# Attention adapter: another order of the small pieces of work in each pipeline slot

## What is computed

```python
# layer 0, "the adapter": 8 heads of 20 columns
hs = mha(x @ Wq, ctx[:, :508] @ Wk, ctx[:, :508] @ Wv)
ca = ctx[:, 508:]                                  # the last 4 context rows
q1 = einsum('btc,th->bch', ca, Wq_ca)[:, indices]
hs1 = mha(q1, x, x)
hs2 = mha(hs1 @ Wq, ca @ Wk_ca, ca @ Wv_ca)
x = (hs + hs2) @ Wout + b_out + x
# layer 1: 20 heads of 64 columns
x = attn(ln(x), ln(x), ...) + x                    # "self"
x = attn(ln(x), ctx, ...) + x                      # "cross"
x = geglu_ff(ln(x), ...) + x
```

## Time and profile before

| | |
|---|---|
| median of 3 runs | 1473.61 us (1472.61 to 1474.12) |
| the profiled execution: its own time | 1475.56 us |
| the profiled execution: span | 1473.8 us |
| mean granted PE clock, whole span | 0.929 |
| adapter | 0 to 335.6 us of the span |
| steady part of the adapter | about 62 to 318 us |

### The profile page before, as it was taken

One profiled execution on the slowest core, in us unless ns is written; L12 is line 12 of the kernel. 1 busy time (PEld: TensorE's weight loads), 2 busy tenths in 40 slices (PEclk: granted clock), 3 DMA queues, 4 the chain that ended last, 5 costly groups with the idle time before them and its releaser, 6 DMA issues. The chain is left out here.

```text
span 1473.8 us, 38650 instructions
## 1 busy us (share of the span) xinstructions
PE 1360.7 (92%) x16460; PEld 1169.2 (79%) x16460; DVE 1025.4 (70%) x1902; ACT 748.2 (51%) x1356; POOL 751.0 (51%) x510
## 2 busy tenths in 40 slices
PE   4989899885999999999979999999999999999597
PEld 3777777764888898889857888888888888888587
DVE  4577777746777867786657777777777767665485
ACT  2356565552555554555425545454555555554264
POOL 2266777565434443444514545454555555455364
PEclk9588888967999999999978999999999999999699
DMA  5001110002000000000010000000010000000000
GB/s 131 12 10 46 47 32 2 2 2 65 2 2 2 2 2 2 2 2 2 2 39 7 2 7 2 7 2 7 2 45 2 2 2 2 2 2 2 12 15 23
DMA packets 31955, 20.33 MB, mean 14 GB/s; under 512 B 21414, under 2 KB 30314, under 8 KB 31786
## 3 DMA queue, kind: packets, MB, share of 16 engines
q1 hardware_dynamic: 31786, 17.86, 4.7%
HBM read 16.54 MB, written 1.31 MB: 12 GB/s over the span
## 5 line engine op out<-in xcount | busy, mean ns | idle before, releaser
L507 POOL TENSOR_TENSOR cross_probs_l<-cross_probs 128x1024 f16<-128x1024 f32 x160 | 303.6, 1897 | 276.5 <-ACT cross_probs L578 276.2
L578 ACT ACTIVATE cross_probs<-cross_score 128x1024 f32<-128x1024 f32 x160 | 163.9, 1024 | 249.9 <-PE cross_score L820 249.9
L507 POOL TENSOR_TENSOR self_probs_l<-self_probs 128x1024 f16<-128x1024 f32 x80 | 151.5, 1894 | 204.0 <-ACT self_probs L578 203.6
L675 DVE TENSOR_REDUCE cross_maxima<-cross_max 128x2 f32<-128x1024 f32 x160 | 194.6, 1216 | 7.4 <-PE cross_max L796 7.2
L1591 POOL TENSOR_TENSOR ad_probs_l<-ad_probs 128x1024 f16<-128x1024 f32 x64 | 120.8, 1893 | 97.7 <-ACT ad_probs L1668 97.0
L578 ACT ACTIVATE self_probs<-self_score 128x1024 f32<-128x1024 f32 x80 | 82.1, 1027 | 156.8 <-PE self_score L820 156.8
L840 PEld LDWEIGHTS cross_pv<-cross_v_h,cross_probs 128*128 128x128 bf16 x1280 | 116.6, 98 | 33.2 <-issue 28.2
L840 PE MATMUL cross_pv<-cross_v_h,cross_probs 128*128 128x65 bf16 x1280 | 135.3, 196 | 2.6 <-POOL cross_probs_l L507 2.6
L661 DVE TENSOR_TENSOR cross_qk_l<-cross_shared,cross_qk_h 128x256 fp32r<-128x256 f32 (+1 forms) x160 | 87.9, 556 | 69.0 <-ACT cross_qk_h L563 68.8
L841 PE MATMUL cross_pv<-cross_v_l,cross_probs 128*128 128x64 f16 x1280 | 133.9, 194 | 0.0
L842 PE MATMUL cross_pv<-cross_v_h,cross_probs_l 128*128 128x65 bf16 x1280 | 133.5, 193 | 0.0
(11 more groups left out here) (420 smaller groups left out, 4735.5 us busy)
## 6 DMA issues: line engine op xcount, KB each, us to landing
ad_ctx_rows<-in_ctx SPq DMA_DIRECT2D x8, 192.0 KB, 2.8
cross_ctx_rows<-in_ctx SPq DMA_DIRECT2D x8, 192.0 KB, 2.5
sw_raw<-in_L_xattn_wq SPq DMA_DIRECT2D x2, 640.0 KB, 6.2
sw_raw<-in_L_xattn_wk SPq DMA_DIRECT2D x2, 640.0 KB, 4.3
sw_raw<-in_L_xattn_wv SPq DMA_DIRECT2D x2, 640.0 KB, 3.8
cw_raw<-in_L_xattn_wq SPq DMA_DIRECT2D x2, 640.0 KB, 4.1
lr_raw<-in_L_xattn_w_ff SPq DMA_DIRECT2D x2, 640.0 KB
out<-x_rows SPq DMA_DIRECT2D x8, 160.0 KB, 1.9
```

Source lines behind the costliest of these rows:

```text
L507: nc.gpsimd.tensor_tensor(probs_l[:, n % PR, :, :].rearrange("p j k -> p (j k)"), whole, whole.bitcast(BF16)[:, 1::2], ALU.subtract).then_ ...
L578: nc.scalar.activation(probs[:, n % PR, :, :].rearrange("p j k -> p (j k)"), score_bank[:, :], ACT.Exp, scale=SCALE).then_inc(exped, 1)
L675: nc.vector.reduce_max(out, scores, AX.X).then_inc(max_read, 1)
```

## The change

It writes the list of a slot in another order, changes three offsets with it, and gives DVE an order of its own.

- Step 0 now holds two `weigh` groups right behind the scores, then `mt`, `e1`, `k`, `q`, `d1`. The projections come in the first half, `k` ahead of `q`.
- Step 1 begins with the other two `weigh` groups, then `top`, then all other small items, with `ctx` in slot 4b - 3 (it was 4b - 1), `x` in 4b - 4 (4b - 3), `e1` in step 0 of 4b + 9 (step 1 of 4b + 8), `e3` and `out` moved from step 0 to step 1 of their slots.
- DVE's slot is now: maximum of step 0, reads of step 0 (`k`, `q`), maximum of step 1, division, `top`, `s2`, reads of step 1.
- `find_max` waits for the read of `q` in place of `k`, since `q` is now the later one, and `KEPT` is 5.
- `DEFER` equals `SLOTS`, so that the branch `g > DEFER` is never taken: every read is done in the slot of its item.

```diff
@@ -1279,10 +1279,11 @@
     KEY_ROWS = [P] * (KT - 1) + [KEYS - (KT - 1) * P]
     ROUNDS = KT // 2
     MAX, MT, SCORE, WEIGH = 2, 3, 4, 5
-    KEPT = 4
+    KEPT = 5
     PR = 2 * ROUNDS
     UNITS = NB * APAIRS
     SLOTS = APAIRS * (NB - 1) + 11
+    DEFER = SLOTS
     SCALE = float(AD) ** -0.5
     HALF = (slice(0, P // 2), slice(P // 2, P))
     WIDE = AH * CDIM + P - CDIM
@@ -1303,38 +1304,40 @@
             if (b := batch(g, offset)) is not None:
                 out.append((step, (what, b, *n)))
 
+        def groups(step):
+            if (p := pair(g, WEIGH)) is not None:
+                out.extend((step, ("weigh", p, 2 * step + n)) for n in range(2))
+
+        groups(0)
         if (p := pair(g, MT)) is not None:
             out.append((0, ("mt", p)))
+        add(0, "e1", 9)
+        if (p := pair(g, 0)) is not None:
+            out += [(0, ("k", p)), (0, ("q", p))]
+        add(0, "d1", 7)
         add(0, "s2", 8)
-        add(0, "v", 4, 1)
-        add(0, "e3", 9)
-        add(0, "d1", 7)
-        if (b := batch(g, -1)):
-            out.append((0, ("ctx", b)))
-        add(0, "out", 10, 0)
-        add(0, "out", 10, 1)
-        if (p := pair(g, WEIGH)) is not None:
-            out += [(0, ("weigh", p, group)) for group in (0, 1)]
-        if (p := pair(g, 0)) is not None:
-            out += [(1, ("q", p)), (1, ("k", p))]
+        groups(1)
+        add(1, "top", 1, 0)
+        add(1, "top", 2, 1)
         if g < 4:
             out += [(1, key) for key in ([("w", 0), ("w", 1), ("ct",)], [("qk", n) for n in range(4)],
                                          [("g2",), ("vt",)], [("vo",)])[g]]
-        add(1, "top", 1, 0)
-        add(1, "top", 2, 1)
+        add(1, "ot", 9)
+        add(1, "v", 4, 1)
         add(1, "xv", 4)
-        if (b := batch(g, -3)):
-            out.append((1, ("x", b)))
-        add(1, "ot", 9)
-        add(1, "rows", 0)
+        add(1, "out", 10, 0)
         add(1, "mq", 3)
-        add(1, "d2", 7)
-        add(1, "v", 3, 0)
-        add(1, "e1", 8)
-        if (p := pair(g, WEIGH)) is not None:
-            out += [(1, ("weigh", p, group)) for group in (2, 3)]
         add(1, "qs", 4, 0)
         add(1, "qs", 5, 1)
+        add(1, "rows", 0)
+        if (b := batch(g, -3)):
+            out.append((1, ("ctx", b)))
+        if (b := batch(g, -4)):
+            out.append((1, ("x", b)))
+        add(1, "out", 10, 1)
+        add(1, "v", 3, 0)
+        add(1, "d2", 7)
+        add(1, "e3", 9)
         add(1, "qw", 6)
         return out
 
@@ -1726,11 +1729,11 @@
                 what, b = key[0], key[1]
                 j, bank_ = b % 2, shared[order.bank(key)]
                 if what == "q":
-                    dve.wait_ge(qk_hi, b * 2 + 1)
+                    dve.wait_ge(qk_hi, b * 2 + 2)
                     nc.vector.scalar_tensor_tensor(q_s[:, b % KEPT, :], q_t[:, :], const["low_q"], bank_[:, 0:SEQ],
                                                    ALU.mult, ALU.add).then_inc(emptied, 1)
                 elif what == "k":
-                    dve.wait_ge(qk_hi, b * 2 + 2)
+                    dve.wait_ge(qk_hi, b * 2 + 1)
                     nc.vector.scalar_tensor_tensor(k_s[:, b % KEPT, 0:KEYS], k_t[:, :], const["low_k"], bank_[:, 0:KEYS],
                                                    ALU.mult, ALU.add).then_inc(emptied, 1)
                 elif what == "x":
@@ -1850,36 +1853,52 @@
                 nc.vector.tensor_tensor(wo_a[:, 1, :], raw_o[:, 0, :], wo_a[:, 0, :], ALU.subtract)
                 nc.vector.tensor_tensor(wo_b[:, 1, :], raw_o[0:2 * HB, 1, :], wo_b[:, 0, :], ALU.subtract).then_inc(prepared, 1)
 
+            def maximum(p, step):
+                dve.wait_ge(max_filled, p * ROUNDS + step + 1)
+                nc.vector.reduce_max(maxima[:, p % 2, step, :, 0], max_bank[:, :].rearrange("p (j k) -> p j k", j=2)[:, :, 0:KEYS],
+                                     AX.X).then_inc(max_read, 1)
+
+            def normalise(p):
+                dve.wait_ge(pv_done, p + 1)
+                groups = pv_bank[:, 0:4 * AV]
+                nc.vector.reciprocal(recip[:, :], groups.rearrange("p (g d) -> p g d", d=AV)[:, :, AD]).then_inc(recip_ready, 1)
+                dve.wait_ge(recip_ready, p + 1)
+                head = p % APAIRS * 2
+                out = attn[p // APAIRS % 2][:, :, head * AD:(head + 2) * AD].rearrange("p t (h d) -> p h t d", h=2)
+                nc.vector.tensor_tensor(out, groups.rearrange("p (h t d) -> p h t d", h=2, t=QT)[:, :, :, 0:AD],
+                                        recip[:, :].rearrange("p (h t) -> p h t", h=2)[:, :, :, None].to_broadcast([P, 2, QT, AD]),
+                                        ALU.mult).then_inc(attn_ready, 1)
+
+            def units(g, step):
+                for at, key in items(g):
+                    if at != step or key[0] in ("weigh", "mt", "d1", "e1", "qs", "xv", "s2", "top"):
+                        continue
+                    if key[0] in SETUP:
+                        set_up(key)
+                    else:
+                        extra(key)
+
             def slot(g):
-                for step in range(ROUNDS):
-                    if (p := pair(g, MAX)) is not None:
-                        dve.wait_ge(max_filled, p * ROUNDS + step + 1)
-                        nc.vector.reduce_max(maxima[:, p % 2, step, :, 0], max_bank[:, :].rearrange("p (j k) -> p j k", j=2)[:, :, 0:KEYS],
-                                             AX.X).then_inc(max_read, 1)
-                    for at, key in items(g):
-                        if at != step or key[0] in ("weigh", "mt", "d1", "e1", "qs", "xv"):
-                            continue
-                        if key[0] in SETUP:
-                            set_up(key)
-                        elif key[0] == "s2":
-                            second_softmax(key[1])
-                        elif key[0] == "top":
-                            _, b, n = key
-                            dve.wait_ge(top_filled, b * 2 + n + 1)
-                            nc.vector.reduce_max(top_q[:, CDIM + 4 * n:CDIM + 4 * n + 4],
-                                                 max_bank[0:CDIM, :].rearrange("p (h k) -> p h k", h=4), AX.X).then_inc(top_read, 1)
-                        else:
-                            extra(key)
-                if (p := pair(g, WEIGH)) is not None:
-                    dve.wait_ge(pv_done, p + 1)
-                    groups = pv_bank[:, 0:4 * AV]
-                    nc.vector.reciprocal(recip[:, :], groups.rearrange("p (g d) -> p g d", d=AV)[:, :, AD]).then_inc(recip_ready, 1)
-                    dve.wait_ge(recip_ready, p + 1)
-                    head = p % APAIRS * 2
-                    out = attn[p // APAIRS % 2][:, :, head * AD:(head + 2) * AD].rearrange("p t (h d) -> p h t d", h=2)
-                    nc.vector.tensor_tensor(out, groups.rearrange("p (h t d) -> p h t d", h=2, t=QT)[:, :, :, 0:AD],
-                                            recip[:, :].rearrange("p (h t) -> p h t", h=2)[:, :, :, None].to_broadcast([P, 2, QT, AD]),
-                                            ALU.mult).then_inc(attn_ready, 1)
+
+                p = pair(g, MAX)
+                if p is not None:
+                    maximum(p, 0)
+                if g > DEFER:
+                    units(g - 1, 1)
+                units(g, 0)
+                if p is not None:
+                    maximum(p, 1)
+                if (v := pair(g, WEIGH)) is not None:
+                    normalise(v)
+                for n in range(2):
+                    if (b := batch(g, 1 + n)) is not None:
+                        dve.wait_ge(top_filled, b * 2 + n + 1)
+                        nc.vector.reduce_max(top_q[:, CDIM + 4 * n:CDIM + 4 * n + 4],
+                                             max_bank[0:CDIM, :].rearrange("p (h k) -> p h k", h=4), AX.X).then_inc(top_read, 1)
+                if (b := batch(g, 8)) is not None:
+                    second_softmax(b)
+                if g < DEFER or g == SLOTS - 1:
+                    units(g, 1)
 
             dve.wait_ge(shapes_in, 16)
             extra(("ctx", 0))
@@ -2059,7 +2078,7 @@
             def find_max(g, step, p):
                 at = p % KEPT
                 if step == 0:
-                    pe.wait_ge(emptied, order.read(("k", p)))
+                    pe.wait_ge(emptied, order.read(("q", p)))
                     after(pe, top_read, extra_fills(g, 1))
                 after(pe, max_read, p * ROUNDS + step)
                 for j, half in enumerate(HALF):
```

## The result

The changed kernel takes 1482.18 us in the median (20 runs, 1470.72 to 1488.18), the one before 1469.50 us (20 runs on the same chip, 1468.26 to 1474.26). The ratio is 1.0076, with a 95% interval of 1.0061 to 1.0092: **slower by 0.8%**, where a gain of 0.3% was forecast. The time lies within the range that was given (1453 to 1486) and beside the rival "the new stall pulls the clock down" (1482.6 us). An execution more than 1.5% above the fastest of its kernel is left out of a ratio: one of four in the second part of experiment 6, two of twelve in experiment 8. What follows compares the two profiled executions, spans of 1483.2 and 1473.8 us; their own times, 1485.02 and 1475.56 us, lie 2.8 and 6.1 us above the medians, so they differ by 9.5 us where the medians differ by 12.7. The adapter ends at 345.8 in place of 335.6 us, 10.2 us later; all that comes behind it is 0.8 us shorter.

What follows compares the result with a forecast made beforehand. No engine was taken as full: PE and DVE wait for each other in turn. The terms -20 + 14 + 2 + 1.5 - 2.5 + 0.6 = -4.4 us took 1473.6 to 1469.2 us, range 1453 to 1486.

Steps and rivals of the forecast that it cites:

- the new stall pulls the clock down: Rival: stalls before `top`, twice a batch, lower PE's clock; 9 us slower, 1482.6 us; chance 0.35.
- The sum of items 1 to 6: Whole kernel: waits removed and added come to -4.4 us, with about 32% of the stretch at 1.2 GHz.
- item 4: Weight pieces on POOL: four of seven fall into slots where POOL has little room left; +1.5 us, bounds 0 and 8.
- its deciding point, a clock of 0.81: Granted clock in the stretch where 6% more at the low level eats up the 4.4 us gain.
- A clock that leaves 0.84 by more than 0.03: Sign of being wrong: the granted clock moving that far in either direction.
- a stall above 1.6 us: Sign of being wrong: PE waiting at `top` longer than the upper bound of 1.6 us.
- PE's total idle time falls in my account: Argument against the slower case: PE, idle for 23.2 us from 62 to 318 us, would idle less.
- Item 1: PE's waits of `d2`, `e1`, `rows` and `find_max` go, `score` behind `qs` stays at 6.1 us; -20 us.
- Item 2: PE at `top` waits for the second maximum, 14 times, 1.0 us on average; +14 us, bounds +7 and +22.
- Item 3: Shorter slots of g mod 4 = 3, then the next slot's first `weigh` waits for POOL's split; +2 us.
- Items 5 and 6: The start loses `find_max` waits in slots 2 and 3, -2.5 us; at the end `e3` is read last, +0.6 us.
- "Slower": Outcome for the whole kernel: slower than before by more than about 0.2%, 3 us; chance 0.35.

Runs made afterwards that it cites:

- second part of experiment 6: Kernel before with the two `weigh` groups first in each half, nothing else moved: 1505.28 us, ratio 1.0180.
- experiment 8: Changed kernel with DVE's second maximum ahead of `k` and `q`, plus unused matmuls (five in slots with `top`, twelve with `mq`): 1465.02 us, ratio 0.9935.
- experiment 2: Changed kernel with twelve unused matmuls ahead of the last `weigh` group in slots that have a `top`: 1471.96 us, ratio 1.0000 to the kernel before.
- experiment 3: Changed kernel with the twelve unused matmuls in slots without `top` (g mod 4 = 0 and 3): 1504.53 us, ratio 1.0216 to the kernel before.
- experiment 1: Changed kernel with DVE reading the second maximum ahead of `k` and `q`: 1469.39 us, ratio 0.9989 to the kernel before.
- experiment 9: Changed kernel with DVE's second maximum ahead of `k` and `q` only in slots with `top`: 1454.18 us, ratio 0.9882 to the kernel before.
- Experiment 10: Experiment 9 with DVE's second softmax moved behind the small reads of the second half: 1451.07 us, ratio 0.9874 to the kernel before.
- experiment 4: Changed kernel with `top` as the last item of its slot on PE and DVE: 1487.65 us, ratio 1.0100 to the kernel before.
- experiment 5: Changed kernel with DVE's small reads of the second half deferred by a slot (`DEFER = 5`): 1540.00 us, ratio 1.0453 to the kernel before.

## Why the prediction was wrong

**The step that failed is the sum's clock.** The sum of items 1 to 6 leaves the share of the low clock at 32% and names its change only among the rivals. The granted clock went to 0.79. For the middle piece the shares at 1.2 GHz are 2 x (1 - 0.84) x 175.2 = 56 us before and 2 x (1 - 0.80) x 179.2 = 72 us after, for the last piece 26 and 51 us, and for the first 18 and 13 us, 35 us more in all. At the prediction's own price of 0.27 us for each, these are 9.5 us of time. Added to the forecast of -4.4 they give +5.1, and with the wait for `v`, 4.2 where item 4 had 1.5, +7.8; the adapter's end moved by 10.2, so 2.4 us stay open. The price holds on like slots of the kernel before: slot 17, with 10 us at the low clock, takes 11.5 us and slot 21, all at full clock, 8.9, which is 0.26 for each.

The rival had the mechanism, and its deciding point, a clock of 0.81, was passed. That its number is so near (1482.6 against 1482.2 us) is in part luck: it was a loss of 9 us set upon 1473.6 us for the kernel before, where the medians now differ by 12.7 upon 1469.5, and it counted on a longer stall that didn't come. A clock that leaves 0.84 by more than 0.03 and a stall above 1.6 us were the prediction's own signs of being wrong; both came. What spoke against it, "PE's total idle time falls in my account", failed: it rose from 23.2 to 27.3 us.

That the new stall is what pulls the clock down was argued there; experiments 2 and 3 show it for the middle piece. For the last piece they don't. In the changed kernel the clock falls at 310.5 us and stays low to the adapter's end, for 35 us, in the kernel before for 20; with the stall filled (2) it is still 33 us, and with it shortened 38 (1) and 34 (9). So 2 to 3.4 of the 7.6 us that the last piece loses stay when the stall is gone, and what keeps the clock low there is open. With one profile of each kernel part of it may be chance, and the changed kernel's runs do spread over 17 us.

**Item 1, waits that go (-20).** Right for `d2`, `e1` and `find_max`; and `score`, left at 6.1 us, lost most of its wait as well. Of the 23 us, 21 went, where 17 was read. But more came than items 2 to 4 held against it: 14.9 us at `top`, 4.2 for `v`, 3.2 for splits and 2.3 for the copies of `mt`, 24.6 us in place of 17.5.

**Item 2, the wait at `top` (+14, bounds 7 and 22).** Right in place, number and size: 14 waits, 14.9 us, most of them 1.0 to 1.3 us at full clock (1.2 said) and 0.3 to 0.7 at the low one (0.6 said). One, 2.30 us, passes the bound of 1.6: in slot 14 DVE reads `k` 1.33 us after the start of the second `find_max`, not 0.25, since I counted `k`'s cast from its matmuls and left out what ACT has ahead of it, here a weight piece. A stall that was forecast to 0.9 us in all was still the cause of the loss, because its price was taken as its length alone.

**Item 3, POOL's splits (+2).** 3.2 us in seven waits of at most 0.5: right. That slots of g mod 4 = 3 would take 6 us was wrong: in the five batches they take 8.0 to 8.3 us. The low clock isn't all of it, since they still take 7.0 us in experiment 9.

**Item 4, weight pieces (+1.5, bounds 0 and 8).** Mis-sized: one piece costs 4.2 us, by way of DVE's product behind it and POOL. Experiment 10 shortens that slot by 1.7 us.

**Items 5 and 6.** The start gained 1.5 us by slot 10, where 2.5 was said. The end was said to lose 0.6 us; the piece lost 7.6, and its idle time fell by 0.5, so all of it is clock. Everything behind the adapter stayed, as said.

**The chances.** "Slower" had 0.35, though the trace of before spoke for it, as the fall behind the gap of 1.2 us in the earlier trace rows does. Read in half microseconds it has 11 falls from 62 us on, each within 2.5 us behind a gap of 0.5 to 1.2 us, four of them behind one of its six gaps of 1.2 us; behind the one at 159.25 the clock stayed up, so a gap makes a fall likely and not sure. The change adds two such gaps to a batch for one. I weighed the sum of the idle time, where what each gap does to the clock decided.

## What to carry to other kernels

On an engine that works in order, put the read that another engine is about to wait for ahead of reads that nobody needs yet, and decide it slot by slot: here that turns a loss of 0.8% into a gain of 1.2% (experiment 9). Count a cast or a hand-over from the queue of the engine that does it, not from when its input is there. When PE idles, price the gap twice, once by its length and once by the clock behind it, and put the clock into the sum.

## What was unexpected of the hardware

- Twelve unused matmuls in each stall made the kernel 10 us faster (clock 0.79 to 0.91); the same twelve in slots without it made it 22 us slower. A filled gap in the kernel before raised the clock to 0.89 and left the time where it was.
- A DVE product of 96x32 elements took between 0.19 and 4.72 us in the changed kernel, by what POOL did beside it (up to 5.03 in experiment 1); it was held through the rest of one POOL operation and three more in a row. The Trainium skill (SBUF — State Buffer, SBUF: two separate sides) states that a DVE operation with two SBUF inputs and a GpSimd operation that reads SBUF exclude each other, and that the one that comes second is blocked fully. The rows agree: POOL's addition runs from 166.44 us, the product comes second at 167.10. They also show it blocked for more than one operation's length, and why it wasn't let in between them is open.
- The same kernel's runs spread by 17 us in the changed kernel (20 runs). The kernel before spread by 6 us beside them and by 14 us (23 runs, 1462.49 to 1476.89) beside experiments 1, 2, 4 and 5. What makes the spread is open: the changed kernel's fastest run has the highest mean clock, 0.950, but its slowest ones have 0.93, more than the 0.92 of those at 1480 us.
